# Attention with int8 feed-forward on one core: row maxima turned on VectorE instead of TensorE, and written to their rows by four DMAs per half

## The reference

```python
def attention(x, mask, Wq, Wk, Wv, b):           # x [B, C, T]
    Q, K, V = proj(Wq), proj(Wk), proj(Wv)        # [B, H, T, 32]
    att = einsum('bhqd,bhkd->bhqk', Q, K) / sqrt(32) + b[0]
    att = att * m + (1 - m) * -1e30               # m = mask over keys
    att = softmax(att, axis=-1)
    y = einsum('bhqk,bhkd->bhqd', att, V)
    return y.transpose(...)                       # [B, C, T]

def ffn(x, weight, w_scale, bias):                # per row of T: int8 quantisation
    scale = max(max|x| over the row, eps) / 127
    q = clip(round(x / scale), -128, 127)
    return float16((q @ weight.T) * scale * w_scale + bias)

out = x + ffn(attention(x, ...), ...)
```

## Time and profile before

| | |
|---|---|
| median of 3 runs | 2441.62 us (2440.1 to 2443.0) |
| the profiled execution's own time | 2440.84 us |
| its span, first to last instruction | 2439.0 us |
| PE busy | 98% of the span |
| DVE, ACT, POOL busy | 64%, 55%, 69% |
| mean granted TensorE clock | 0.993 |
| mean DMA rate | 163 GB/s |

### The profile page before, as it was taken

How to read it: one execution, slowest core, us unless ns; L and a number is a source line. 1 busy time by engine, 2 the same in 40 slices (tenths; PEclk the granted TensorE clock), 3 DMA queues, 4 the chain that set the end, 5 groups by cost and what they waited for, 6 DMA issues and landing times.

```text
span 2439.0 us, 37390 instructions
## 1 busy us (share of the span) xinstructions
PE 2387.2 (98%) x12376; PEld 1341.0 (55%) x12376; DVE 1560.4 (64%) x1683; ACT 1346.3 (55%) x2536; POOL 1672.1 (69%) x677
## 2 busy tenths in 40 slices
PE   8999999997999999999999999999999999999996
PEld 7888888884444444444444444444444444444442
DVE  3311111145777777777777777777777877777771
ACT  3222222214666666666666666666666666666664
POOL 3322223414778888888877888888788888887777
PEclk9999999998999999999999999999999999999999
DMA  6655555365677776777677777666776667776751
GB/s 243 252 200 199 214 193 195 147 211 126 147 160 160 157 157 147 157 159 159 151 159 159 156 160 156 157 151 150 160 160 155 155 150 160 160 155 154 157 111 44
DMA packets 143498, 396.55 MB, mean 163 GB/s; under 512 B 14584, under 2 KB 50424, under 8 KB 127296
## 3 DMA queue, kind: packets, MB, share of 16 engines
q0 software_dynamic: 18144, 132.13, 27.4%
q10 hardware_dynamic: 49312, 130.80, 22.8%
q1 hardware_dynamic: 75968, 132.74, 14.9%
HBM read 161.51 MB, written 100.93 MB: 108 GB/s over the span
## 4 chain that ended last, share of the span: by engine, by line
PE 67%; DMA 4%; issue 2%; POOL 2%; DVE 2%; ACT 0%; SPq 0%; ACTq 0%; POOLq 0%; DVEq 0%
PE score L689 21%; PE pv L716 18%; PE ring L127 18%; PE ring L749 4%; DMA q_stack<-max_lo 4%; PE ring L726 2%; PE ring L729 2%; DVE neg_max L136 1%; PE ring L740 1%; POOL acc L988 1%; PE ring L734 0%; DMA probs<-probs 0%; POOL acc L1000 0%; ACT probs L798 0%; SPq L609 0%
## 5 line engine op out<-in xcount | busy, mean ns | idle before, releaser
L798 ACT ACTIVATE probs<-score 128x512 f32<-128x512 f32 x2048 | 1074.7, 604 | 576.4 <-PE score L689 559.5
L136 DVE TENSOR_REDUCE neg_max<-ring 128x1 f32<-128x1024 f32 x1024 | 1208.4, 1220 | 230.8 <-PE ring L127 219.1
L689 PE MATMUL score<-q_stack,k_stack 100*128 100x512 f32 x2048 | 875.8, 429 | 23.9 <-DMA q_stack<-max_lo 16.6
L988 POOL TENSOR_TENSOR acc<-acc,probs 128x2048 f32<-128x2048 f32 x189 | 867.1, 4588 | 26.6 <-DMA probs<-probs 11.9
L127 PE MATMUL ring<-k_stack,q_stack 98*128 98x512 f32 x2048 | 810.6, 396 | 0.3 <-DVE neg_max L136 0.2
L689 PEld LDWEIGHTS score<-q_stack,k_stack 100*128 100x128 f32 x2048 | 387.3, 189 | 504.0 <-ACT probs L798 358.2
L716 PE MATMUL pv<-probs,v_in 128*32 128x512 f32 x4096 | 546.1, 605 | 0.0
L127 PEld LDWEIGHTS ring<-k_stack,q_stack 98*128 98x128 f32 x2048 | 390.8, 191 | 66.6 <-DVE neg_max L136 0.8
L988 POOL TENSOR_TENSOR acc<-probs 128x2048 f32<-128x2048 f32 x63 | 288.8, 4584 | 100.8 <-DMA probs<-probs 100.8
L479 POOL TENSOR_TENSOR q_stack<-x_raw,k_stack 128x1024 fp32r<-128x1024 f32 x28 | 67.7, 2450 | 294.7 <-ACT k_stack L364 294.7
L972 POOL DMA_DIRECT2D probs<-probs x126 | 108.2, 859 | 175.4 <-PE pv L716 168.2
(11 more groups left out here) (95 smaller groups left out, 2026.6 us busy)
## 6 DMA issues: line engine op xcount, KB each, us to landing
probs<-probs POOLq DMA_DIRECT2D x126, 1024.0 KB, 8.0
k_stack<-qk_part ACTq DMA_DIRECT2D x93, 512.0 KB
q_stack<-qk_part ACTq DMA_DIRECT2D x183, 256.0 KB, 5.4
qk_part<-part_hi SPq DMA_DIRECT2D x64, 512.0 KB, 2.6
qk_part<-part_lo SPq DMA_DIRECT2D x64, 512.0 KB, 3.5
v_steps<-v_out SPq DMA_DIRECT2D x64, 256.0 KB, 2.2
res<-x ACTq DMA_DIRECT2D x32, 512.0 KB, 5.7
out<-res SPq DMA_DIRECT2D x64, 256.0 KB, 2.1
```

What stands on the lines that cost most here:

```text
L136: nc.vector.tensor_reduce(neg_max[:, pair // CHUNK, pair % CHUNK:pair % CHUNK + 1], ring[:, :], AX_X, ALU.max, negate=True).then_inc(neg_m ...
L689: pe.matmul(score[score_bank(t)][:, :], k_stack[par][0:ROWS, h, kt * P:(kt + 1) * P], q_stack[par][0:ROWS, half, h, :], start=True, stop=T ...
L798: nc.scalar.activation(probs[:, kt, h, :], score[score_bank(t)][:, :], ACT.Exp).then_inc(exp_done, 1)
L988: nc.gpsimd.tensor_tensor(acc[:, half, :, :], first, probs[:, tile, :, :], ALU.add).then_inc(acc_done, 1)
```

## The change

Step 1 above goes away, and with it its fp32 identity matrix and the semaphore `maxT_done`. The split into two parts is done on the columns as they are, 128x16, in SBUF. ACT writes the high part and DVE the rest into `max_parts`, side by side, so that one half is 128 partitions by 32 columns. DVE turns these in one instruction, a block transpose: each of the four 32x32 blocks (32 queries by 32 columns) is transposed in place. So partition 32g + 16r + c of `max_turned` holds part r of column c (head and query tile) for the 32 queries of block g. SP then issues four DMAs, one for each block g: 32 partitions of 32 elements, which go as 128 B runs into both rows, [2 rows, 4 heads, 4 query tiles, 32 queries]. All four count on `max_rows[chunk]`, so PE now waits for 64 more per step instead of 32.

`high_max`, `low_max` and the new `turn_max` stand at t = 23 and t = 55 as before; the ring buffer is taken only for the sums.

```diff
-        max_hi = sb("max_hi", [CHUNK, 2, P], F32R)
-        max_lo = sb("max_lo", [CHUNK, 2, P], F32R)
-        ident = sb("ident", [P, P], F32)
+        max_parts = sb("max_parts", [P, 2, 2, CHUNK], F32R)
+        max_turned = sb("max_turned", [P, 2, 2 * CHUNK], F32)
...
-        MAX_ROWS = 16 * 2
+        MAX_ROWS = 16 * P // DH
...
             def store_max(par, chunk):
 
-                for part, rows in ((0, max_hi), (1, max_lo)):
-                    dst = q_stack[par][ROW_MAX + part:ROW_MAX + part + 1, chunk, :, :]
-                    sp.dma_start(dst.bitcast(F32), rows[:, chunk, :].bitcast(F32)).then_inc(max_rows[chunk], 16)
+                rows = q_stack[par][ROW_MAX:ROW_MAX + 2, chunk, :, :].rearrange("r h (a g j) -> r h a g j", g=P // DH, j=DH)
+                for g in range(P // DH):
+                    sp.dma_start(rows[:, :, :, g, :].bitcast(F32), max_turned[g * DH:(g + 1) * DH, chunk, :]).then_inc(max_rows[chunk], 16)
...
                 if main:
-                    sp.wait_ge(max_hi_done, 2 * s + 2)
-                    sp.wait_ge(max_lo_done, 2 * s + 2)
+                    sp.wait_ge(max_turn_done, 2 * s + 2)
                     store_max(par, 1)
...
                 elif t in (SUMS_1, SUMS_0):
-                    wait(pe, sums_out, 2 * s + (t == SUMS_0))
-                    if not isinstance(s, int) or s + (t == SUMS_0) < STEPS:
-                        pe.wait_ge(max_lo_done, 2 * s + (2 if t == SUMS_1 else 3))
+                    pe.wait_ge(sums_out, 2 * s + (t == SUMS_0))
...
-            def turn_max(s, chunk, buf):
-                pe.wait_ge(neg_max_done, PAIRS * s + CHUNK * (chunk + 1))
-                pe.transpose(buf[0:CHUNK, N:N + P], neg_max[:, chunk, :], ident[:, :]).then_inc(maxT_done, 1)
...
-                    if t == SUMS_1 and (prev or main):
-                        buf = take_ring(s, par, use)
-                        if main:
-                            turn_max(s, 1, buf)
-                        if prev:
-                            sum_rows(s - 1, 1, buf)
+                    if t == SUMS_1 and prev:
+                        sum_rows(s - 1, 1, take_ring(s, par, use))
...
-            def high_max(s, chunk, buf):
-                act.wait_ge(maxT_done, 2 * s + chunk + 1)
-                wait(act, max_rows[chunk], MAX_ROWS * s)
-                nc.scalar.activation(max_hi[:, chunk, :], buf[0:CHUNK, N:N + P], ACT.Copy).then_inc(max_hi_done, 1)
+            def high_max(s, chunk):
+                act.wait_ge(neg_max_done, PAIRS * s + CHUNK * (chunk + 1))
+                wait(act, max_turn_done, 2 * (s - 1) + chunk + 1)
+                nc.scalar.activation(max_parts[:, chunk, 0, :], neg_max[:, chunk, :], ACT.Copy).then_inc(max_hi_done, 1)
...
+            def low_max(s, chunk):
                 dve.wait_ge(max_hi_done, 2 * s + chunk + 1)
+                dve.wait_ge(neg_max_done, PAIRS * s + CHUNK * (chunk + 1))
+                nc.vector.tensor_tensor(max_parts[:, chunk, 1, :], neg_max[:, chunk, :],
+                                        max_parts[:, chunk, 0, :].bitcast(F32), ALU.subtract).then_inc(max_lo_done, 1)
+
+            def turn_max(s, chunk):
+
+                dve.wait_ge(max_lo_done, 2 * s + chunk + 1)
+                wait(dve, max_rows[chunk], MAX_ROWS * s)
+                nc.vector.transpose(max_turned[:, chunk, :],
+                                    max_parts[:, chunk, :, :].rearrange("p a b -> p (a b)").bitcast(F32)).then_inc(max_turn_done, 1)
```

More of the change, by code:

```diff
@@ L650, in taken @@
                     return 0 <= max_of_slot(s, t)[0] < STEPS
-                return s < STEPS if t == SUMS_0 else 0 <= s <= STEPS if t == SUMS_1 else 0 <= s - 1 < STEPS
+                return 0 <= s < STEPS if t == SUMS_0 else 0 <= s - 1 < STEPS
             def wait_ring(s, use):
@@ L762, in step @@
                     use = ("extra", t)
-                    if t == SUMS_1 and (prev or main):
-                        buf = take_ring(s, par, use)
-                        if main:
-                            turn_max(s, 1, buf)
-                        if prev:
-                            sum_rows(s - 1, 1, buf)
-                    if t == SUMS_0 and (main or ahead):
-                        buf = take_ring(s, par, use)
-                        if ahead:
-                            turn_max(s + 1, 0, buf)
-                        if main:
-                            sum_rows(s, 0, buf)
+                    if t == SUMS_1 and prev:
+                        sum_rows(s - 1, 1, take_ring(s, par, use))
+                    if t == SUMS_0 and main:
+                        sum_rows(s, 0, take_ring(s, par, use))
                     if t == TURN_Q and prev:
@@ L862, in step @@
                     if t == SUMS_0 and ahead:
-                        high_max(s + 1, 0, ring_of(par, ("extra", SUMS_0)))
-            act.wait_ge(const_set, 5)
+                        high_max(s + 1, 0)
+            act.wait_ge(const_set, 4)
             act.wait_ge(stack_set, 4)
@@ L874, in _ @@
             nc.vector.memset(magic[:, 1:2], -MAGIC).then_inc(const_set, 1)
-            def low_max(s, chunk, buf):
+            def low_max(s, chunk):
                 dve.wait_ge(max_hi_done, 2 * s + chunk + 1)
-                nc.vector.tensor_tensor(max_lo[:, chunk, :], buf[0:CHUNK, N:N + P],
-                                        max_hi[:, chunk, :].bitcast(F32), ALU.subtract).then_inc(max_lo_done, 1)
+                dve.wait_ge(neg_max_done, PAIRS * s + CHUNK * (chunk + 1))
[6 more added lines that the diff above has]
+                                    max_parts[:, chunk, :, :].rearrange("p a b -> p (a b)").bitcast(F32)).then_inc(max_turn_done, 1)
             def recip(s, half, buf):
@@ L930, in step @@
                     if t == SUMS_1 and main:
-                        low_max(s, 1, ring_of(par, ("extra", SUMS_1)))
+                        low_max(s, 1)
+                        turn_max(s, 1)
                     if t == 19 and prev:
@@ L947, in step @@
                     if t == SUMS_0 and ahead:
-                        low_max(s + 1, 0, ring_of(par, ("extra", SUMS_0)))
+                        low_max(s + 1, 0)
+                        turn_max(s + 1, 0)
                     if t == SUMS_0 and main:
@@ L957, in _ @@
         def _(pool):
-            for eye in (ident, ident16):
-                nc.gpsimd.memset(eye[:, :], 0.0).then_inc(zeroed, 1)
-            for k, eye in enumerate((ident, ident16)):
-                pool.wait_ge(zeroed, 2)
-                nc.gpsimd.affine_select(out=eye[:, :], in_=eye[:, :], compare_op=ALU.not_equal, fill=1.0, base=0,
-                                        pattern=[[-1, P]], channel_multiplier=1).then_inc(const_set, 1)
+            nc.gpsimd.memset(ident16[:, :], 0.0).then_inc(zeroed, 1)
+            pool.wait_ge(zeroed, 1)
+            nc.gpsimd.affine_select(out=ident16[:, :], in_=ident16[:, :], compare_op=ALU.not_equal, fill=1.0, base=0,
+                                    pattern=[[-1, P]], channel_multiplier=1).then_inc(const_set, 1)
             set_rows(nc, q_stack[1], k_stack[1], stack_set)
```

10 lines of the change are left out of this document (4 added, 6 removed).

## The result

The changed kernel takes 2651.4 us, median of four runs (2648.5 to 2656.9), against 2442.3 us for the kernel before on the same chip: a ratio of 1.086, 95% interval 1.084 to 1.0879. That is slower by 209 us, as the prediction said in direction, but nearly four times the 53 us that it forecast, and beyond the range (2436 to 2545).

A forecast was written before the change was run, and what follows sets the result against it. The prediction took PE as the bound, tied in some steps with writing the max rows, and summed 2440.8 - 6.8 (transposes) + 59 (late landing at t = 32) + 1 (before the first step) = 2494 us; range 2436 to 2545.

The forecast's parts named there:

- What bounds the kernel: PE bounds it; at t = 32 the max rows land under 0.2 us before the score; DMAs land in issue order.
- taking turns between the queues: Another way to put the last small transfer behind all three loads at t = 32, 3.1 us late; not adopted.
- The transpose leaves PE: 0.22 us each; the 31 at t = 55 gain 6.8 us, those at t = 23 count zero.
- The split and the turn: DVE's max_lo and block transpose take 0.45 us against 0.28, so SP starts 0.2 us later at t = 23.
- the 0.15 to 0.3 that were to show the prediction right: Confirming sign: two DVE instructions, the new max_lo and the block transpose, of 0.15 to 0.3 us.
- Four DMAs at t = 55: Hidden: rows there by 1433.2 or 1434.1, against 1434.9 for the next t = 0; no cost.
- Four DMAs at t = 23: Transfer 4 lands behind ACT's load 2, so t = 32 starts 1.9 us late; 59 us over 31 steps.
- a rival of mine at 0.20: All three loads ahead of transfer 4: t = 32 starts 3.1 us late, price 96 us, total 2531 us; chance 0.20.
- the spread over 2 engines: Each new transfer runs on 2 DMA engines: estimated 0.7 us behind the addition, 21 us more, left out.
- My rivals: One load ahead, 2453 us (0.18); all three, 2531 (0.20); loads don't hold transfers, 2431 (0.16); no change, 2441 (0.06).
- The two signs that were to show the prediction wrong: Last transfer landing within 0.5 us of POOL's addition, or its issue over before ACT's second load is issued.
- Before the first step: One identity less on POOL, two more SP issues and 0.2 us on DVE: taken as +1 us.

The follow-up runs named there:

- e4: Kernel before, with each of its two max-row transfers per half split in two of 8 rows, four in all: 2550.8 us, ratio 1.0443.
- e9: Changed kernel with ACT's three loads of q_stack at t = 28, 29, 30, behind SP's fourth issue: 2431.7 us, ratio 0.9967.
- e1: Changed kernel with ACT's three loads of q_stack at t = 33, 34, 35 instead of 24, 25, 26: 2411.8 us, ratio 0.9886.
- e6: Changed kernel with only two of the four transfers per half from the third step on, leaving out part of the work: 2478.0 us, ratio 1.0151.
- e8: Changed kernel with each of its four transfers split by row, eight per half of 16 partitions: 2668.1 us, ratio 1.0933.
- e3: Kernel before with the new path at t = 55 alone; t = 23 keeps PE's transpose and two transfers: 2443.7 us, ratio 1.0011.
- e7: Kernel before with the new path at t = 55 alone and ACT's three loads at t = 33 to 35: 2418.1 us, ratio 0.9908.

## Why the prediction was wrong, by its own steps

**What bounds the kernel: right, with the order of landing too strict.** PE is the bound and the landing of the max rows at t = 32 is the second. That the DMAs of that stretch land in the order of their issue holds roughly: e4 has transfer 4 between loads 2 and 3, the changed kernel behind load 3, and e9 ahead of all. But the packets of SP's and ACT's queues lie side by side. The prediction set aside taking turns between the queues because max_lo landed 0.7 us ahead of load 1; that row does not decide it, and for the changed kernel it stays a possible part of the cause.

**The transpose leaves PE: right in sign, too small.** I took 0.22 us for each, its piece of the chain. PE's stream became shorter by 0.34 us at t = 55 and 0.28 at t = 23. That the half at t = 23 is worth nothing while the landing sets t = 32 was right.

**The split and the turn: right where it counts.** The block transpose takes 0.21 us (0.25 taken), max_lo's successor 0.165 us at t = 23 (0.2 taken). At t = 55 it takes 0.9 to 1.0 us, outside the 0.15 to 0.3 that were to show the prediction right, and is hidden (see the last section).

**Four DMAs at t = 55: right.** No wait at t = 0 (11.01 - 4.88 us from t = 56, as before 11.35 - 5.22). The cover was less safe than it was made to look: slow issues had been paired with the shortest landing and quick ones with the median. Slow issues with the median landing give 1431.4 + 4.1 = 1435.5, behind the 1434.9 of t = 0. The issues there take 0.61 us, so it did not come to that.

**Four DMAs at t = 23: the step that failed.** "Transfer 4 lands behind load 2, at 1463.9 [...] 1.9 us late" had three faults.
- The issues. I allowed 0.58 to 1.36 us for the third and fourth and chose load 2, since most of that range ends there. They took 1.22 and 1.30. The 1.36 of max_lo was no peculiarity of the second place in the queue; every issue of SP but the first is slow there, in e1 also without a load near. That puts transfer 4 level with load 3 or behind it (3.19 against 3.09 us behind SP's first issue in the median): 3.1 instead of 1.9, a rival of mine at 0.20. An issue that the trace shows slow at one spot should be taken slow for all that follow it there.
- The landings were taken as fixed. I read the landing times of before and asked only behind which one the fourth transfer falls. But the packets of the transfers lie among those of the loads, and load 3 lands 1.96 us later behind SP's first issue in the median step, 1.87 in the step above. The prediction set aside the spread over 2 engines, an estimate of 0.7 us, because no row of before showed one. e6, with two transfers of the new form, has load 3 0.8 us later and t = 32 1.2; e8, with as many runs of the same 128 B on 16 engines, has load 3 at 10.68, 0.2 us later. So the narrow spread is the likelier cause and not the small runs. It is not isolated: e8 also has only half of the runs issued ahead of load 3. The delay of 1.9 us is in any case no term of my sum. Together, in the step above, 3.0 + 1.9 + 0.3 = 5.2 us.
- The clock. A wait that ran to 5.5 us lowered it, at 2.8 us a step (2.50 + 0.26). Nothing of it is in the sum. My rivals too ended with the landing. And it would have mattered at the forecast's own 1.9 us of wait: after waits from 1.7 to 2.5 us e4 lost 1.2 us a step, which for 31 steps is an estimate of 37 us on top of the 59. Shorter waits cost less often. In e6, waits from 1.3 to 2.2 us stand in 27 of the steps, and in 6 of them the products behind are slow, by 1.5 us each; its median step has none of it (3.08 from t = 32 to t = 36).

In sum 31 x (-0.62 + 5.17 + 2.76) = 227 us by the median step, of which the run shows 209. The two signs that were to show the prediction wrong did not appear, and it was wrong all the same: both looked for a shorter wait, none for a longer one. That the sign of the change was right is not luck, since the wait is where it was forecast; of its size the sum had only a part.

**Before the first step:** the first step's wait grew by 1.5 us (15.7 against 9.7 + 4.5), where I had 1.

**What stays open.** Why an issue on SP or ACT takes 1.2 to 1.4 us in this stretch. e1 excludes the loads as its cause, and e9's 0.76 us and e1's 0.33 us show that it fades with time. It is not simply that one of POOL's additions is in flight. At t = 55 of e1 one is, too: it is issued at 1405.5 and lands at 1414.5, and SP's four issues, from 1413.0 on, are quick:

```profile
L608 SPq DMA_DIRECT2D q_stack<-max_turned x4: 610/611/619, 1413.0 to 1414.9; - x4
```

There the first issue starts 7.5 us behind that of the addition; at t = 23, where three of four are slow, it is 3.3 us. So the time since the addition's issue goes with it, but no run moved the additions. Open as well is how much of load 3's delay is the spread over few engines and how much the turns between the queues.

## What to carry to other kernels

A transfer that ends a critical wait should be counted by its issue and by what is already queued when the last part is issued, and splitting it moves that last part back past everyone else's transfers; here 0.66 us of gain a step became 7.3 of loss, and moving three unrelated loads by nine slots brought both back, 2411.8 us against 2441.0, the best version here. When a forecast adds a wait on TensorE, the price has a second term, which e4 shows behind waits of 1.7 to 2.5 us already: look at what the granted clock did after waits of that length. Test a small edit also with its neighbour out of the way (e3 against e7), or a real gain reads as none.

## What the runs showed of the hardware that I had not expected

A wait of 5.5 us on TensorE cost 2.8 us more at the 1.2 GHz level, and 20 useless matmuls in the wait gave 65.8 us back over the run. Waits near 2 us (e4) cost 1.2 us on the average.

VectorE's subtraction into `max_parts`, 128x16, waits for GpSimd. At t = 23 it takes 165 ns; the median of all 64 is 914 and the longest 4325. Its group, and DVE and POOL at t = 55:

```profile
L861 DVE TENSOR_TENSOR max_parts<-neg_max,max_parts x64: 165/914/4325, 568.3 to 2582.7; 128x16 fp32r<-128x16 f32 x64
```

```profile
1457.82 1.01 DVE L861 TENSOR_TENSOR max_parts<-neg_max,max_parts 128x16 fp32r<-128x16 f32 x1
```

```profile
1457.64 1.16 POOL L1006 TENSOR_TENSOR res<-res,half 128x512 f32<-128x512 f32 x1
```

DVE's ends at 1458.83, POOL's at 1458.80, though POOL's started first. In e3 the pair ends at 1431.49 and 1431.46. In the changed kernel all 33 of these subtractions that take over 0.5 us end 0.03 us behind an instruction of POOL; the other 31 take less than 0.2 us. The section "Who interferes with whom" of the Trainium skill's page "SBUF — State Buffer" says that a VectorE instruction with two inputs in SBUF contends with a GpSimd instruction that reads SBUF, over a port pair that one of them holds exclusively; the ends, 0.03 us apart, agree. In the kernel before the first input was in PSUM. At t = 55 it cost nothing, since it is hidden there. In the first steps, where it took 3.0 to 4.3 us, I did not price it. In a kernel whose VectorE is the bound, moving an operand from PSUM to SBUF could cost more than the operation; no run here has such a bound.
